# Running the maximum scores three units ahead, with the maxima sent as two transfers of one row

## The chip, the core and the metric

The kernel runs on one core of a Trainium2 chip: TensorE (PE) for matrix products, VectorE (DVE), ScalarE (ACT) and GpSimd (POOL) for elementwise work, and SyncE (SP) and ACT's queue to issue transfers. The metric is device time in microseconds for one execution, median of several runs.

## What is computed

32 sequences of 128 tokens with 128 features go through a self attention, a cross attention to a second sequence, a gate and a gated MLP, with a padding mask on the keys of both attentions. There are 16 heads of 8 features.

```python
def masked_attn(q, k, v, valid_keys):
    scores = jnp.einsum('bhqd,bhkd->bhqk', q, k) / math.sqrt(HD)
    scores = jnp.where(valid_keys[:, None, None, :], scores, jnp.finfo(scores.dtype).min)
    return jnp.einsum('bhqk,bhkd->bhqd', jax.nn.softmax(scores, axis=-1), v)
# tokens: rmsnorm, film, q/k/v, rope on q and k
tokens = tokens + merge_heads(masked_attn(q, k, v, valid)) @ out_w.T + out_b
# cross: query = rmsnorm(tokens), keys and values from rmsnorm(seq_tokens)
attended = merge_heads(masked_attn(cq, ck, cv, svalid)) @ mha_out_w.T + mha_out_b
update = attended * valid_rows
gate = jax.nn.sigmoid(jnp.concatenate([tokens, update], axis=-1) @ gate_w.T + gate_b)
tokens = tokens + gate * update
g, val = jnp.split(rmsnorm(tokens, ffn_norm_w) @ gu_w.T + gu_b, 2, axis=-1)
out = tokens + jax.nn.silu(g) * val @ down_w.T + down_b
```

## The kernel before

**Tiling.** The 32 sequences form 8 groups of 4. Each group passes one self phase and one cross phase, so there are 16 phases, in the order of the table `ORDER` (L35: SELF 0 to 3, CROSS 0, SELF 4, CROSS 1 and so on, the last three being CROSS 5, 6 and 7). A phase has four *units* (one sequence each, 64 in all), a unit has four *quarters* of four heads (256 in all), and two units make a *pair* (32 in all).

**Order.** Every engine runs its own program, and all of them walk through the same loop over quarters, `for t in range(FIRST, LAST)`, with `n, q = divmod(t, 4)`. What an engine does in a quarter is written out by hand through due times: `s_prep(g)` and `c_prep(g)` start the preparation of a group's self and cross phase, `top_time(m)` is the quarter in which the maxima of pair m are turned, `post(g, step)` and `mlp(g)` place what follows the attention. An engine takes its work strictly in this order; semaphores hold it until its inputs are there.

**Attention.** q and k are cut into three bfloat16 parts each, and the nine products of parts are stacked along the partitions: `q_st` and `k_st` (`st`, three sets, one per phase in turn) have 72 rows of parts, a row for the mask, and in `q_st` two rows for the maxima. The stacks are filled by transfers from SP (`stack`, L658; three for each part, 18 in a phase). The parts themselves (`part_q`, `part_k`) are written by ACT (`keep_hi`, L872, and `keep_mid`, L876) and POOL. `keep_hi` waits (`parts_free`) until the transfers of an earlier phase have landed, since it overwrites what they read.

Scores are made twice. `max_scores(n, q)` (L356, matmuls L366) makes scores with queries on the partitions in `ps_a`; DVE reduces them to a maximum for each query and head (`maxima`, L1087) in `top`. This runs `LEAD` units ahead, 4 before the change: in quarter t PE makes the maximum scores of quarter t + 16. `prob_scores(n, q)` (L378, L386) makes them again with keys on the partitions in `ps_b`, the two rows of the maxima being part of the contraction, so that the maximum is already taken off; ACT's exponential (`exps`, L902) writes `probs`, and `weigh` (L390, L403) multiplies them with the values one unit later.

**The maxima of a pair** go this way: DVE splits them, negated, into two bfloat16 parts (`split_tops`, L1096 and L1098, `top_part`); PE turns them (`turn_tops`, L374) into a PSUM bank; ACT copies them (`keep_top`, L888) to `top_t`, 32 partitions (2 parts by 16 heads) of 256 queries; ACT's queue issues the transfer (`top_rows`, L895) that lays them as two rows of `q_st`. `prob_scores` waits for it at the first quarter of every second unit, that is at quarter 8m for pair m. In the kernel before, the split of pair m is at quarter 8m-8, the turn at 8m-5 (8m-7 for pair 0), copy and transfer at 8m-4, the copy ahead of that quarter's exponential and the transfer behind it.

**DVE beside this.** At the last quarter of every second unit `take_pair` (L1105, L1107) takes a pair's output; `divide_pair`, `keep_v`, `rope` and the norms have their own quarters. **ACT beside this:** in each quarter, after its exponential, copies and squares (L828), L863, L922 and L924. **PE:** within a quarter it does `weigh` (third quarter of a unit), `turn_tops`, `max_scores`, `prob_scores`, then the quarter's products.

Of the kernel before, what the change touches and what calls it, by code (L numbers as in the profile page):

```python
# [14 lines left out]
H = 16  # L15
# [14 lines left out]
TOPS = 2  # L30
# [9 lines left out]
POS = {one: p for p, one in enumerate(ORDER)}  # L40
LEAD = 4
SETS = 3
# [5 lines left out]
def s_prep(g):  # L48
    return 16 * (POS[SELF, g] - 2) - 8 - 6 * (g == 1)

# [23 lines left out]
def top_time(m):  # L74
    return 8 * m - (7 if m == 0 else 5)

# [33 lines left out]
def build(nc, x, side, cond, mask, anw, qkv_w, qkv_b, out_w, out_b, film_w, film_b, sqw, snw, in_w, in_b,  # L110
          mo_w, mo_b, gate_w, gate_b, fnw, gu_w, gu_b, down_w, down_b, cos_t, sin_t, ident_t, out):
    with ExitStack() as ctx:
# [189 lines left out]
        def _(pe):  # L302
# [75 lines left out]
            def prob_scores(n, q):  # L378
                p, b = divmod(n, NG)
                i = p % SETS  # L380
                if q == 0:
                    pe.wait_ge(top_in[n // 2 % 2], 16 * (n // 4 + 1))
                wait(pe, exp_done, NQ * n + q - 1)
                for j in range(QH):
                    h = QH * q + j
                    mm = pe.matmul(ps_b[q % 2][:, j * S:(j + 1) * S], st[1][i][0:R_END, h, b * S:(b + 1) * S],  # L386
                                   st[0][i][0:R_END, h, b * S:(b + 1) * S], start=True, stop=True)
                mm.then_inc(b_done, 1)
# [419 lines left out]
        def _(act):  # L808
# [76 lines left out]
            def keep_top(m):  # L885
                src = full_in(act, ("top", m))
                wait(act, top_in[m % 2], 16 * (m // 2))
                act.activation(top_t[:, m % 2, :], src[:, :].bitcast(BF16)[0:TOPS * H, 0:2 * S], ACT.Copy  # L888
                               ).then_inc(taken_sem(("top", m)), 1)

            def top_rows(m):

                p, pair = divmod(m, 2)
                taken(act, ("top", m))
                act.dma_start(st[0][p % SETS][R_MAX:R_END, :, pair * 2 * S:(pair + 1) * 2 * S], top_t[:, m % 2, :]  # L895
                              ).then_inc(top_in[m % 2], 16)

# [64 lines left out]
            for t in range(FIRST, LAST):  # L962
                n, q = divmod(t, 4)
                for m in range(PAIRS):
                    if t == top_time(m) + 1:
                        keep_top(m)
                if 0 <= n < UNITS:
                    exps(n, q)
                for m in range(PAIRS):
                    if t == top_time(m) + 1:  # L970
                        top_rows(m)
                for g in range(G):
# [64 lines left out]
        def _(dve):  # L1037
# [198 lines left out]
            for t in range(FIRST, LAST):  # L1236
                n, q = divmod(t, 4)
                if n % 2 == 0 and q == 0 and 0 <= (n + 2) // 2 < PAIRS:
                    split_tops((n + 2) // 2)
                if 0 <= n + LEAD < UNITS:  # L1240
# [90 lines left out]
```

## Time and profile before

| | |
|---|---|
| median of 3 runs | 515.77 us (515.37 to 520.08) |
| the profiled execution | 517.94 us, span 516.1 us |
| PE busy | 442.1 us, 86% of the span |
| DVE busy | 350.1 us, 68% |
| ACT busy | 290.4 us, 56% |
| POOL busy | 190.8 us, 37% |
| mean granted TensorE clock | 0.937 |

The profile shows one execution. "Busy" is the time in which an engine executes; the wait of an engine is told by the instruction that ends it and by what released it. PE's granted clock is a share of 2.4 GHz: 1.0 is that level, 0.5 is the lower level of 1.2 GHz, and a value between them is a mean over a stretch that had both. The first 41 us of the span are preparation; from there to 61 us PE makes the maximum scores of the first four units and prepares other groups; the last phase's scores end at 479 us, and the rest is the MLP of the last group.

### The profile page before, as it was taken

To read this page: it belongs to the slowest core of one execution; us is meant where nothing else is said; L and a number is where in the kernel's file an instruction comes from. 1 tells how busy PE (TensorE), PEld (TensorE's weight loads), DVE (VectorE), ACT (ScalarE), POOL (GpSimd) and SP (SyncE) were. 2 spreads that over 40 slices of the span, in tenths; PEclk is the share of its full clock that TensorE was granted. 3 is DMA by queue.
4 is the path that set the end of the run, shared out by engine and by line. 5 is a ranking of instruction groups with operands and counts; after the bars stand their busy time and mean duration, and the time that the engine had idled before them with its cause. 6 is when DMAs were issued, how large, how long until landed. Compare 5 with 4: busy or idle time off the path is not lost.

```text
span 516.1 us, 13226 instructions
## 1 busy us (share of the span) xinstructions
PE 442.1 (86%) x5219; PEld 308.3 (60%) x5219; DVE 350.1 (68%) x655; ACT 290.4 (56%) x644; POOL 190.8 (37%) x184
## 2 busy tenths in 40 slices
PE   3546889878897986999989988999999969999897
PEld 2115375756675664666577655866586748565664
DVE  2326655878885896698677866767748856856565
ACT  4321364577566664777576648486636744556243
POOL 4451140614433163528381828254542542000010
PEclk9975778899997999799999999999989999999999
DMA  3355442354353445344443443425140320000001
GB/s 77 87 174 174 131 122 88 100 162 151 100 162 107 140 121 153 103 128 121 131 137 108 117 140 97 153 67 163 43 149 25 98 92 3 23 3 22 22 1 42
DMA packets 62942, 52.04 MB, mean 101 GB/s; under 512 B 3803, under 2 KB 61728, under 8 KB 62880
## 3 DMA queue, kind: packets, MB, share of 16 engines
q1 hardware_dynamic: 60050, 49.07, 32.2%
q10 hardware_dynamic: 2830, 2.12, 1.4%
q8 instruction: 42, 0.69, 0.6%
q14 instruction: 20, 0.16, 0.1%
HBM read 8.55 MB, written 2.11 MB: 21 GB/s over the span
## 4 chain that ended last, share of the span: by engine, by line
PE 52%; DVE 11%; DMA 10%; ACT 8%; issue 8%; SPq 5%; POOL 4%; ACTq 1%; DVEq 0%; POOLq 0%
PE ps_o L403 8%; PE ps_a L366 7%; PE ps_g L320 7%; PE ps_b L386 6%; PE ps_g L461 5%; SPq L658 4%; DMA k_st<-part_k 4%; DVE top L1087 4%; PE ps_g L444 4%; PE ps_g L353 3%; DMA q_st<-top_t 3%; ACT probs L902 2%; DMA s_in<-in_fside_BxSxS 1%; ACT turned_in L838 1%; PE ps_g L418 1%
## 5 line engine op out<-in xcount | busy, mean ns | idle before, releaser
L1087 DVE TENSOR_REDUCE top<-ps_a 128x4 f32<-128x512 f32 x256 | 169.6, 680 | 106.1 <-PE ps_a L366 104.8
L902 ACT ACTIVATE probs<-ps_b 128x512 f32<-128x512 f32 x256 | 151.3, 595 | 143.6 <-PE ps_b L386 139.5
L366 PE MATMUL ps_a<-k_st,q_st 73*128 73x128 bf16 x1024 | 105.0, 228 | 27.8 <-DMA k_st<-part_k 15.0
L366 PEld LDWEIGHTS ps_a<-k_st,q_st 73*128 73x128 bf16 x1024 | 69.8, 101 | 79.5 <-issue 59.9
L386 PE MATMUL ps_b<-q_st,k_st 75*128 75x128 bf16 x1024 | 102.0, 223 | 9.4 <-ACT probs L902 7.5
L386 PEld LDWEIGHTS ps_b<-q_st,k_st 75*128 75x128 bf16 x1024 | 69.6, 99 | 18.5 <-issue 9.2
L403 PE MATMUL ps_o<-probs,v_pad 128*32 128x128 f32 x2048 | 73.3, 287 | 0.0
L403 PEld LDWEIGHTS ps_o<-probs,v_pad 128*32 128x32 f32 x2048 | 55.3, 115 | 24.1 <-issue 14.7
L728 POOL TENSOR_TENSOR f<-f 128x4 f32<-128x4 f32 x16 | 16.6, 1038 | 98.8 <-DVE f L1136 98.8
L320 PE MATMUL ps_g<-norm,w_t 128*128 128x512 f32 x66 | 37.1, 647 | 1.2 <-DVE hid L1178 1.2
L320 PE MATMUL ps_g<-turned_in,w_t 128*128 128x512 f32 x48 | 30.3, 717 | 5.0 <-ACT turned_in L838 4.8
L444 PE MATMUL ps_g<-norm,w_t 128*128 128x512 f32 x56 | 30.1, 620 | 3.3 <-DVE quotient L1132 2.6
L461 PE MATMUL ps_g<-w_t,hid 128*128 128x128 f32 x224 | 27.4, 276 | 0.0
L765 POOL TENSOR_SCALAR unit_th<-unit_th 128x512 f32<-128x512 f32 x16 | 9.9, 620 | 45.0 <-ACT unit_th L922 45.0
L461 PEld LDWEIGHTS ps_g<-w_t,hid 128*128 128x128 f32 x224 | 26.0, 192 | 0.0
L922 ACT ACTIVATE unit_th<-ps_g,half_g_b 128x512 f32<-128x512 f32 x22 | 15.1, 686 | 14.3 <-PE ps_g L444 14.3
L1105 DVE STREAM_TRANSPOSE turned<-ps_o 128x512 f32<-128x512 f32 x32 | 22.6, 706 | 0.3 <-PE ps_o L403 0.3
L749 POOL TENSOR_TENSOR part_k<-full_k,part_k 128x512 bf16<-128x512 f32 x14 | 16.2, 1158 | 17.8 <-ACT part_k L876 17.7
L353 PE MATMUL ps_g<-w_t,turned_in 128*128 128x128 f32 x128 | 21.9, 325 | 0.2 <-ACT top_t L888 0.2
L718 POOL TENSOR_TENSOR f<-f 128x4 f32<-128x4 f32 x16 | 16.4, 1024 | 14.5 <-DVE f L1043 13.9
L744 POOL TENSOR_TENSOR full_k<-full_k,part_k 128x512 f32<-128x512 f32 x14 | 16.4, 1168 | 13.3 <-ACT part_k L872 13.3
L768 POOL TENSOR_TENSOR hid<-hid,unit_th 128x512 f32<-128x512 f32 x16 | 20.3, 1268 | 1.3
(197 smaller groups left out, 677.6 us busy)
## 6 DMA issues: line engine op xcount, KB each, us to landing
q_st<-part_q SPq DMA_DIRECT2D x126, 128.0 KB
k_st<-part_k SPq DMA_DIRECT2D x120, 128.0 KB
x_in<-in_x SPq DMA_DIRECT2D x16, 256.0 KB, 4.5
q_st<-hid SPq DMA_DIRECT2D x18, 128.0 KB
s_in<-in_fside_BxSxS SPq DMA_DIRECT2D x8, 256.0 KB, 5.7
out<-t SPq DMA_DIRECT2D x8, 256.0 KB, 2.3
k_st<-hid SPq DMA_DIRECT2D x12, 128.0 KB
swap_q<-part_q SPq DMA_DIRECT2D x8, 128.0 KB, 2.3
```

Of the source, the lines that this page charges most:

```text
L320: pe.matmul(to[:, :], w, rhs, start=True, stop=True).then_inc(done, 1)
L353: mm = pe.matmul(to[:, b * D:(b + 1) * D], src[:, b * S:(b + 1) * S], w, start=True, stop=True)
L366: mm = pe.matmul(ps_a[q % 2][:, j * S:(j + 1) * S], st[0][i][0:R_MAX, h, b * S:(b + 1) * S], st[1][i][0:R_MAX, h, b * S:(b + 1) * S], star ...
L386: mm = pe.matmul(ps_b[q % 2][:, j * S:(j + 1) * S], st[1][i][0:R_END, h, b * S:(b + 1) * S], st[0][i][0:R_END, h, b * S:(b + 1) * S], star ...
L403: mm = pe.matmul(ps_o[32 * c:32 * c + 32, u * 256:(u + 1) * 256].rearrange("p (b r q) -> p r b q", r=2, q=32)[:, r], v_pad[p % 2][:, b, at ...
L444: pe.matmul(to[:, :], w_t[:, W_GU + j, :], norm3[:, :], start=True, stop=True).then_inc(done, 1)
L461: mm = pe.matmul(to[:, b * D:(b + 1) * D], hid[:, j, b * S:(b + 1) * S], w_t[:, W_DOWN + j, :], start=False, stop=j == 3 and b == NG - 1)
L658: sp.dma_start(st[r][p % SETS][product:R_MASK:PRODUCTS, :, :], parts(r, p)[:, o, :]).then_inc(stacked[r][p % 2], 16)
L768: pool.tensor_tensor(hid[:, j, :], hid[:, j, :], unit_th[:, :], ALU.mult).then_inc(g_mul, 1)
L902: act.activation(probs[:, n % 2, q * T:(q + 1) * T], ps_b[q % 2][:, :], ACT.Exp, scale=SCALE).then_inc(exp_done, 1)
L1087: dve.tensor_reduce(top[:, n // 2 % 2, n % 2, QH * q:QH * (q + 1)], ps_a[q % 2][:, :].rearrange("p (h k) -> p h k", h=QH), AX.X, ALU.max). ...
L1105: dve.transpose(turned[:, :], ps_o[:, :]).then_inc(o_taken, 1)
```

## The change

The maximum scores run three units ahead (`LEAD = 3`). The preparation of SELF 2 is moved by four quarters to keep its place to the maximum scores that read it. The split of pair m goes from quarter 8m-8 to 8m-4, ahead of that quarter's maxima, the turn to 8m-3 for every pair, copy and transfer to 8m-2. The transfer is cut into two of one row each, 16 partitions of `top_t` for each, and both are issued ahead of the quarter's exponential. The waits count two transfers for each pair.

```diff
-LEAD = 4
+LEAD = 3
 def s_prep(g):
-    return 16 * (POS[SELF, g] - 2) - 8 - 6 * (g == 1)
+    return 16 * (POS[SELF, g] - 2) - 8 - 6 * (g == 1) + 4 * (g == 2)
 def top_time(m):
-    return 8 * m - (7 if m == 0 else 5)
+    return 8 * m - 3
...
                 if q == 0:
-                    pe.wait_ge(top_in[n // 2 % 2], 16 * (n // 4 + 1))
+                    pe.wait_ge(top_in[n // 2 % 2], 16 * TOPS * (n // 4 + 1))
...
                 src = full_in(act, ("top", m))
-                wait(act, top_in[m % 2], 16 * (m // 2))
+                wait(act, top_in[m % 2], 16 * TOPS * (m // 2))
...
                 taken(act, ("top", m))
-                act.dma_start(st[0][p % SETS][R_MAX:R_END, :, pair * 2 * S:(pair + 1) * 2 * S], top_t[:, m % 2, :]
-                              ).then_inc(top_in[m % 2], 16)
+                for part in range(TOPS):
+                    act.dma_start(st[0][p % SETS][R_MAX + part:R_MAX + part + 1, :, pair * 2 * S:(pair + 1) * 2 * S],
+                                  top_t[H * part:H * part + H, m % 2, :]).then_inc(top_in[m % 2], 16)
...
                 for m in range(PAIRS):
                     if t == top_time(m) + 1:
                         keep_top(m)
+                        top_rows(m)
                 if 0 <= n < UNITS:
                     exps(n, q)
-                for m in range(PAIRS):
-                    if t == top_time(m) + 1:
-                        top_rows(m)
...
-                if n % 2 == 0 and q == 0 and 0 <= (n + 2) // 2 < PAIRS:
-                    split_tops((n + 2) // 2)
+                if n % 2 == 1 and q == 0 and 0 <= (n + 1) // 2 < PAIRS:
+                    split_tops((n + 1) // 2)
```

## Rows read from the trace of the kernel before

**Rows 1.** Waits of PE from 61 us on: us, times, longest
```profile
PE ps_b L386 <- ACT probs L902: 7.5, 16, 0.9
PE ps_a L366 <- DMA k_st<-part_k: 7.1, 2, 4.4
PE ps_a L366 <- DVE top L1087: 6.5, 11, 1.6
PE ps_a L366 <- issue: 3.9, 1, 3.9
PE ps_g L425 <- ACT norm L931: 3.5, 5, 0.8
...
PE ps_b L386 <- DMA q_st<-top_t: 1.9, 3, 1.1
```

**Rows 2.** The chain that ended last, one piece: start us, us, what
```profile
119.79 3.46 DMA q_st<-top_t
```

**Rows 3.** Timeline behind two stack waits: start us, us, instruction [idle before]
```profile
157.72 0.63 ACT L872 ACTIVATE part_k<-full_k 128x512 bf16<-128x512 f32 x1 [2.35 <-DMA k_st<-part_k]
...
160.93 0.63 PE L386 MATMUL ps_b<-q_st,k_st 75*128 75x128 bf16 x4
...
206.67 0.63 ACT L872 ACTIVATE part_k<-full_k 128x512 bf16<-128x512 f32 x1 [3.47 <-DMA k_st<-part_k]
...
209.88 0.63 PE L386 MATMUL ps_b<-q_st,k_st 75*128 75x128 bf16 x4
```

**Rows 4.** Stretch behind the third wait: length, busy time by engine, PE's clock, DMA
```profile
424.00:427.00 3.00, 3.00 (x46) 2.38 (x45) 1.21 (x2) 2.24 (x4) 1.41 (x2) 0.55 0.02 5
```

**Rows 5.** Instructions on `top` (ns min/median/max), and the page's group of maximum scores
```profile
L1087 DVE TENSOR_REDUCE top<-ps_a x256: 627/683/693, 41.4 to 450.1; 128x4 f32<-128x512 f32 x128
L1096 DVE TENSOR_SCALAR top_part<-top x32: 171/182/933, 49.0 to 450.9; 128x32 bf16<-128x32 f32 x32
L1098 DVE SCALAR_TENSOR_TENSOR top_part<-top,top_part x32: 191/193/1075, 49.2 to 451.1; 128x32 bf16<-128x32 f32 x32
...
L366 PE MATMUL ps_a<-k_st,q_st 73*128 73x128 bf16 x1024 | 105.0, 228 | 27.8 <-DMA k_st<-part_k 15.0
```

**Rows 6.** Timeline around pair 5, by ACT, DVE and PE
```profile
119.41 0.36 ACT L888 ACTIVATE top_t<-ps_g 32x256 bf16<-32x256 bf16 x1
119.67 0.57 ACT L902 ACTIVATE probs<-ps_b 128x512 f32<-128x512 f32 x1
...
120.49 0.60 ACT L902 ACTIVATE probs<-ps_b 128x512 f32<-128x512 f32 x1 [0.25 <-issue]
...
119.04 0.11 DVE L1043 TENSOR_SCALAR f<-f 128x4 f32<-128x4 f32 x1
...
118.17 0.40 PE L366 MATMUL ps_a<-k_st,q_st 73*128 73x128 bf16 x4
```

**Rows 7.** Timeline at pair 1 (ACT, PE) and pair 30 (DVE, PE), first and last late
```profile
71.37 0.19 ACT L828 ACTIVATION_READ_ACCUMULATOR junk<-x_in 128x1 f32 x1
...
73.48 0.39 PE L386 MATMUL ps_b<-q_st,k_st 75*128 75x128 bf16 x4
...
444.83 0.63 DVE L1087 TENSOR_REDUCE top<-ps_a 128x4 f32<-128x512 f32 x1
...
444.60 0.39 PE L366 MATMUL ps_a<-k_st,q_st 73*128 73x128 bf16 x4
```

**Rows 8.** Issue of the maxima (ns min/median/max), and a mask row at 255 us (us to landing)
```profile
L895 ACTq DMA_DIRECT2D q_st<-top_t x32: 621/621/697, 50.3 to 459.7; - x32
...
k_st<-mask_rows SPq DMA_DIRECT2D x1, 16.0 KB, 2.2
```

**Rows 9.** Timeline around pair 22, by ACT and PE
```profile
338.55 0.22 ACT L828 ACTIVATION_READ_ACCUMULATOR junk<-s_in 128x1 f32 x1
...
339.40 0.38 PE L386 MATMUL ps_b<-q_st,k_st 75*128 75x128 bf16 x4 [0.69 <-ACT probs L902]
```

## The prediction

> **What bounds the kernel now.** I read the page's busy times first (PE is the busiest engine, by the table above), then PE's waits from 61 us on, where the first probability scores are made. The reader is to see in them that little is left idle, and where [rows 1]. Three long waits stand out, all at the first maximum scores of a phase (`max_scores` with b == 0, q == 0, which waits for the stacked operands): two of 7.1 us together, the longer 4.4 us, and one of 3.9 us named "issue". The third has the same place (first quarter of the last phase) and nothing else to wait for, so I take it to be the same wait. The row of the maxima itself costs little: 1.9 us in three waits, and when PE waits for it, it lands 3.46 us after its issue [rows 1, 2]. The rest is short and spread: 7.5 us on ACT's exponentials, 6.5 us on DVE's maxima, 3.5 us on a square.
>
> A quarter t below is one turn of the loops; pair m needs its maxima at quarter 8m.
>
> **What the change gives.** Maximum scores run 12 quarters ahead of the probability scores and no longer 16, while the stacking of a phase stays where it was (but for SELF 2, moved by 4). So each phase's stacks get four quarters, some 6 us, more before the first reader. All three waits are shorter than that.
> - The 3.9 us wait: nothing else waits for those stacks, all of it goes. 3.9.
> - The wait of 4.4 us: ACT's L872 (the next phase's copy) waits for the same landing until 206.67 and ends at 207.30; the exponential behind it then ends at 207.9, and the probability scores two quarters later need it. They began at 209.88 and can't begin before 207.8 [rows 3]. 2.1.
> - Its sister of 2.7 us (7.1 less 4.4): the same, L872 at 157.72, its exponential done at 158.9, the scores it holds at 160.93 [rows 3]. 2.0.
> - A small one at the fourth phase turns into a wait for the maxima; 0.2.
> That is 8.2 us. After such a wait PE runs at the lower level for a while: granted clock 0.55 in the 3 us after the last, so 1.35 us lost [rows 4]. I give all of that back once and half of it, 0.9 in all, for the two waits that only shrink: 2.3.
> - Start: four quarters of maximum scores, paced by DVE at 0.68 us each while nothing else runs, no longer stand ahead of the first probability scores: 2.7. They come at the end instead, where PE is full, at 105.0/256 = 0.41 us a quarter [rows 5]: minus 1.6. Net 1.1. The preparation of SELF 2, moved by four quarters, leaves the start and comes back just behind it; nothing.
> Gain in all: 8.2 + 2.3 + 1.1 = 11.6 us.
>
> **What it costs.** The time from the last maximum to the first reader of the row shrinks from 8 quarters to 4.
> 1. *The split.* `split_tops(m)` now runs at quarter 8m-4, right behind the quarter whose maxima it needs; in that same quarter DVE also has `take_pair` (L1105, L1107). `turn_tops` on PE comes one quarter later, at 8m-3, where it had three. Behind it in PE's order wait that quarter's maximum and probability scores. The split itself takes 0.18 + 0.19 us, 0.42 with the handover [rows 5]. Pair 5: DVE is free at 119.1, the split would be there at 119.5, PE reached that quarter at 118.17: 1.3 us late [rows 6]. The last such is pair 30: DVE takes the next maximum at 444.83, the split would be there at 445.25, PE is there at 444.60: 0.65 [rows 7].
> 2. *The landing.* The copy `keep_top` goes to quarter 8m-2, behind everything ACT has in 8m-3, and the transfers are issued at once, ahead of the exponential. From the end of ACT's work of 8m-3 it takes 0.39 (copy, to the issue) + 0.55 (first issue) + the landing of the second. The before kernel's issue takes 0.62 [rows 8]; for a one-row one I estimate 0.55. The landing lies between 2.2 us, which a one-row transfer on a quiet queue takes (the mask row) and 3.46 (the maxima beside stacks) [rows 2, 8]. I take 2.3, near the lower end: the transfer has ACT's queue to itself. So 3.24 us after ACT is free. Pair 22: ACT ends with 8m-3 at 338.77, so 342.0; the scores began at 339.40: 2.6 late [rows 9]. Pair 1, the first late one: ACT is through at 71.56; but copy and issue no longer stand ahead of the exponentials before it, which held them up by 0.26 us (copy at 119.41, exponential at 119.67) and by some 0.3 (idle 0.25 for the issue) [rows 6], so 70.96; landing 74.2 against 73.48: 0.7 late [rows 7].
>
> The Trainium skill (DMA: Bandwidth & Descriptors, "Why a DMA increments its semaphore by 16 and not by 1") says that a transfer is spread over the largest number of engines up to 16 that divides both outermost sizes: two for the old one (32 rows to 2), sixteen for each of the new ones; it speaks for a landing near the lower bound, as I take it by the rows.
>
> Done for all 31 pairs in this way (later of the two paths, less what the exponentials gain), 22 are late, pair 1 the first and pair 30 the last, by 30.0 us in sum: 12.7 from the split, 17.3 more from the landing. The two issues hold the exponential of 8m-2 by about 1.5 us, but its result, copy + issues + 0.6 = 2.1 us after ACT is free, is there before the landing; while that cover stands it costs nothing more. A late pair isn't lost whole: PE has 17.5 us of short waits [rows 1] which the others can fall into while PE stands. I let a third be swallowed: 20.0 us remain.
>
> **The sum.** 516.1 - 11.6 + 20.0 = 524.5 for the profiled span. The profiled execution itself took 517.94, the median of the runs is 515.77; I put the difference on the median: 515.77 + 8.4 = 524.2 us.
>
> **Rivals.**
> - *Stalls mostly swallowed, same.* If half of the 30.0 goes, 15 - 11.6 = +3.4, 519.2. For it: the late pairs cluster in the first half, where PE's short waits are; against: after 250 us PE is full and pairs 20, 22 and 26 are late by 2.3 to 2.6 each. 0.25.
> - *Faster.* DVE, freed from lagging by PE's pauses, has the split ready when PE comes, and the row lands in 2 us. It decides from 0.53 us for each of 22 late pairs downward (11.6/22), and is faster by over 1% below 0.3. At 0.2 each: 4.4 - 11.6 = -7.2, 508.6. For it: the waits for the stacks are certain and the lateness is an inference; against: ACT's work ahead of the copy is real, and 2.3 is already the low end. 0.20.
> - *The rows land no sooner than now.* With 3.3 us, just under the 3.46 of the row [rows 2], the same list sums to 50.4: 33.6 - 11.6 = +22, 537.8. For it: the stacks load the DMA engines in most of the span. 0.07. The Trainium skill says so for halves (DMA: Bandwidth & Descriptors, "Rules for kernel authors"): don't cut a transfer into two over disjoint partitions, they serialize on the same engines. No run yet shows it for these shapes.
> - *The stack waits stay*, because L872 keeps ACT waiting for them and all else behind it [rows 3]: the gain falls to the last wait, its clock and the start, 3.9 + 1.4 + 1.1 = 6.4: +13.6, 529.4. 0.08.
> My forecast: 0.40.
>
> **How the numbers follow.** Faster 0.20; within 1% (about what a measurement of this kernel can tell from no change) 0.25; slower 0.40 + 0.07 + 0.08 = 0.55. The forecast alone, with landings of 2.3 to 2.8 us (sum 38.8, so up to 530) and a swallowed share of a third to 45%, spans 520 to 530. The range goes down to half of the faster case and up past the case of the stacks: 509 to 533; below it I leave some 0.1, above it 0.1.
>
> **What would show it.** Right: PE's waits for `k_st` after 61 us fall under 4 us in sum and the 3.9 us one is gone; `turn_tops` (L374) appears as a waiter on DVE's `top_part` with some 8 to 13 us; PE's L386 waits on the transfer of `top_t` for 8 to 20 us; first probability scores near 54 us and not 61. Wrong: L374 and L386 wait under 7 us together, then it is faster; or `k_st` waits as long as before; or PE's clock falls after the new stalls, which I count at nothing.

## The result and the profile after

| | before | changed |
|---|---|---|
| median | 515.57 us (4 runs) | 601.83 us (4 runs) |
| ratio, 95% interval | | 1.164 [1.157, 1.170] |
| profiled execution | 517.94 us, span 516.1 | 600.95 us, span 599.2 |
| PE busy in the span | 442.1 us | 475.4 us |
| PE idle from 61 us on, pauses over 50 ns | 44.7 us | 90.1 us |
| mean granted TensorE clock | 0.937 | 0.880 |

The direction was forecast, the size was not: 86 us lost where 8.4 were predicted, far above the range. The table says where they are. PE ran the same 5219 instructions and was busy 33.3 us longer; its pauses grew by 45.4 us. Together that is 78.7 of the 83.1 us of span. Ratios, here and below, leave out executions that took over 1.5% longer than the fastest of their kernel.

The first lines of the page of the changed kernel, its row of the granted clock and its queues (q10 is ACT's, with the rows of the maxima; before it had 2830 packets):

```profile
span 599.2 us, 13258 instructions
PE 475.4 (79%) x5219; PEld 329.2 (55%) x5219; DVE 357.0 (60%) x655; ACT 290.0 (48%) x644; POOL 190.1 (32%) x184
...
PEclk9775788869996889897889889888879989979999
...
q10 hardware_dynamic: 3790, 2.13, 1.4%
```

PE's waits in the changed kernel from 61 us on (line, what ended the wait, us in total, times, longest), to be read against [rows 1]:

```profile
PE ps_g L374 <- DVE top_part L1097: 18.4, 17, 2.1
PE ps_b L386 <- DMA q_st<-top_t: 18.1, 13, 2.9
PE ps_g L353 <- DVE hid L1177: 10.3, 6, 3.0
PE ps_g L374 <- DVE norm L1141: 5.5, 4, 1.6
PE ps_g L444 <- DVE hid L1177: 4.2, 2, 2.2
PE ps_b L386 <- ACT probs L903: 4.1, 4, 2.0
PE ps_g L439 <- ACT full_k L863: 4.1, 3, 1.4
PE ps_a L366 <- DVE top L1086: 3.7, 9, 0.8
```

Three things are to be seen. The three waits for the stacks of [rows 1] are gone. The first two rows are the two new waits that I predicted: the turn on the split, the scores on the landing of the rows. And the third, fourth, fifth and seventh rows stand in no line of the prediction. They end when DVE or ACT has read out an earlier result in `ps_g`, the PSUM banks that all small products share: `hid` is DVE's read of an MLP product, `norm` DVE's second half of a normalisation, `full_k` ACT's read of a key product. PE waits there for a bank and not for data. Before, L353, the values' product, waited 0.6 us in the whole kernel.

A stretch of the changed kernel, PE alone (start, duration, instruction, in brackets the idle time before it and its releaser):

```profile
352.90 0.27 PE L374 MATMUL ps_g<-ident_b,top_part 128*128 128x128 bf16 x2 [1.55 <-DVE norm L1141]
...
354.98 2.05 PE L439 MATMUL ps_g<-t,w_t 128*128 128x512 f32 x2 [1.36 <-ACT full_k L863]
356.82 1.91 PE L440 MATMUL ps_g<-upd,w_t 128*128 128x512 f32 x2
358.66 1.94 PE L403 MATMUL ps_o<-probs,v_pad 128*32 128x128 f32 x32
```

The granted clock over it (stretch; its length; busy time and count of PE, PEld, DVE, ACT, POOL; PE's clock; DMA share; GB/s):

```profile
351.00:355.00 4.00, 1.09 (x12) 0.63 (x11) 3.29 (x7) 1.41 (x5) 0.45 (x1) 0.83 0.19 54
355.00:360.00 5.00, 5.00 (x32) 2.37 (x36) 0.57 (x1) 0.37 (x3) 0.00 (x0) 0.50 0.03 7
360.00:363.00 3.00, 3.00 (x39) 2.05 (x32) 1.50 (x3) 1.81 (x5) 0.55 (x1) 0.92 0.00 1
```

Two pauses for banks, 1.55 and 1.36 us, in a stretch in which PE was busy 1.09 of 4 us, and behind them 5.9 us of matmuls (2.05, 1.91, 1.94) at a granted clock of 0.50, the lower level of 1.2 GHz; the same three groups took 1.10, 1.02 and 1.08 us in the kernel before. So the two pauses of 2.9 us were followed by 2.7 us more of PE's time for the same work. This is how 33 us of busy time come from the same instructions.

### The profile page after: what moved, and what is told of

The parts are those of the page before. It is cut to its first block, busy times and chain, and to the rows that moved or that the text cites. A ratio compares the mean times of both kernels' runs of the same rounds, so it can differ in the third digit from the quotient of the medians.

```text
span 599.2 us, 13258 instructions
## 1 busy us (share of the span) xinstructions
PE 475.4 (79%) x5219; PEld 329.2 (55%) x5219; DVE 357.0 (60%) x655; ACT 290.0 (48%) x644; POOL 190.1 (32%) x184
## 4 chain that ended last, share of the span: by engine, by line
PE 50%; DVE 17%; issue 8%; DMA 8%; ACT 7%; POOL 4%; ACTq 3%; SPq 2%; DVEq 0%; POOLq 0%
PE ps_o L403 9%; DMA q_st<-top_t 7%; PE ps_g L320 6%; PE ps_a L366 6%; DVE top L1086 6%; PE ps_b L386 6%; PE ps_g L461 4%; PE ps_g L444 4%; PE ps_g L353 3%; DVE turned L1104 2%; SPq L658 2%; PE ps_g L338 1%; DMA t<-in_L_cond_down_w 1%; DVE top_part L1097 1%; PE ps_g L439 1%
## 5 line engine op out<-in xcount | busy, mean ns | idle before, releaser
L386 PE MATMUL ps_b<-q_st,k_st 75*128 75x128 bf16 x1024 | 106.3, 229 | 26.3 <-DMA q_st<-top_t 21.8
L366 PE MATMUL ps_a<-k_st,q_st 73*128 73x128 bf16 x1024 | 108.8, 234 | 14.8 <-DMA k_st<-part_k 8.6
L366 PEld LDWEIGHTS ps_a<-k_st,q_st 73*128 73x128 bf16 x1024 | 73.2, 104 | 60.3 <-issue 47.2
L386 PEld LDWEIGHTS ps_b<-q_st,k_st 75*128 75x128 bf16 x1024 | 73.0, 103 | 35.1 <-DMA q_st<-top_t 24.5
L403 PE MATMUL ps_o<-probs,v_pad 128*32 128x128 f32 x2048 | 83.3, 313 | 0.0
L403 PEld LDWEIGHTS ps_o<-probs,v_pad 128*32 128x32 f32 x2048 | 62.1, 125 | 29.3 <-issue 17.9
L320 PE MATMUL ps_g<-norm,w_t 128*128 128x512 f32 x68 | 39.1, 661 | 0.7 <-ACT probs L903 0.7
L353 PE MATMUL ps_g<-w_t,turned_in 128*128 128x128 f32 x128 | 26.5, 373 | 14.5 <-DVE hid L1177 10.3
L444 PE MATMUL ps_g<-norm,w_t 128*128 128x512 f32 x56 | 32.2, 658 | 4.8 <-DVE hid L1177 4.2
L353 PEld LDWEIGHTS ps_g<-w_t,turned_in 128*128 128x128 f32 x128 | 23.0, 269 | 15.8 <-DVE hid L1177 9.0
L374 PE MATMUL ps_g<-ident_b,top_part 128*128 128x128 bf16 x64 | 9.4, 232 | 27.3 <-DVE top_part L1097 19.0
L374 PEld LDWEIGHTS ps_g<-ident_b,top_part 128*128 128x128 bf16 x64 | 4.1, 99 | 39.7 <-DVE top_part L1097 27.5
L749 POOL TENSOR_TENSOR part_k<-full_k,part_k 128x512 bf16<-128x512 f32 x14 | 16.2, 1156 | 29.9 <-ACT part_k L876 29.8
L718 POOL TENSOR_TENSOR f<-f 128x4 f32<-128x4 f32 x16 | 16.4, 1024 | 17.8 <-DVE f L1042 17.3
```

The costliest lines, as they stand in the source:

```text
L320: pe.matmul(to[:, :], w, rhs, start=True, stop=True).then_inc(done, 1)
L353: mm = pe.matmul(to[:, b * D:(b + 1) * D], src[:, b * S:(b + 1) * S], w, start=True, stop=True)
L366: mm = pe.matmul(ps_a[q % 2][:, j * S:(j + 1) * S], st[0][i][0:R_MAX, h, b * S:(b + 1) * S], st[1][i][0:R_MAX, h, b * S:(b + 1) * S], star ...
L403: mm = pe.matmul(ps_o[32 * c:32 * c + 32, u * 256:(u + 1) * 256].rearrange("p (b r q) -> p r b q", r=2, q=32)[:, r], v_pad[p % 2][:, b, at ...
L444: pe.matmul(to[:, :], w_t[:, W_GU + j, :], norm3[:, :], start=True, stop=True).then_inc(done, 1)
L718: pool.tensor_tensor(r[:, :], ms[:, :], minus_half[:, :], ALU.pow).then_inc(root_set, 1)
```

## The experiments

"Lead 4" below means `LEAD = 4` and the old due time of SELF 2. Each diff is against the kernel it is named for; a ratio is to the kernel before on the same chip. The kernel before had medians of 512.3, 518.1, 514.9 and 513.8 us beside the four groups of runs, which ran on three chips; where kernels of two groups are compared, or a single execution is given, some 5 us are not certain. Kernels without the landing's wait or without the turn leave out a part of the computation; they serve for timing alone.

### One part alone: the cut

Kernel before, only the transfer cut in two, both still at quarter 8m-4 behind the exponential.

```diff
-                act.dma_start(st[0][p % SETS][R_MAX:R_END, ...], top_t[:, m % 2, :]).then_inc(top_in[m % 2], 16)
+                for part in range(TOPS):
+                    act.dma_start(st[0][p % SETS][R_MAX + part:R_MAX + part + 1, ...],
+                                  top_t[H * part:H * part + H, m % 2, :]).then_inc(top_in[m % 2], 16)
```

> The kernel before with only the transfer cut into two of one row each, still at quarter 8m-4 and behind the exponential; lead 4. Theory A (lateness in the chain of the maxima makes the loss, the transfers themselves are cheap): within 1% of before, perhaps 1 to 2 us faster since PE's three waits for the maxima shrink. Theory B (thirty-two more issues on ACT and 16 instead of 2 engines for each disturb the stacks): slower by 2% or more.

Measured: 515.16 against 512.29 us, ratio 1.003 [0.997, 1.008]. Where nobody waits for the rows, the cut costs nothing that can be measured.

### Turn and landing late, lead 4

Changed kernel with lead 4; the turn at 8m-3 and copy and transfers at 8m-2 ahead of the exponential, as changed, but the split at its old quarter 8m-8.

```diff
-LEAD = 3
+LEAD = 4
...
-                if n % 2 == 1 and q == 0 and 0 <= (n + 1) // 2 < PAIRS:
-                    split_tops((n + 1) // 2)
+                if n % 2 == 0 and q == 0 and 0 <= (n + 2) // 2 < PAIRS:
+                    split_tops((n + 2) // 2)
```

> Lead 4, split at quarter 8m-8 as before, but turn at 8m-3 and copy and two transfers at 8m-2 ahead of the exponential, as in the changed kernel. Theory A1 (the late landing is the main part): 550 us or more, PE waits over 15 us for the transfer of top_t. Theory A2 (the split right behind its maxima is the main part): under 535 us. Theory C (the later turn changes which PSUM bank each product gets, and the bank waits are the loss): L353 and L439 wait on DVE and ACT as in the changed kernel, some 20 us.

Measured: 576.98 us (one execution; the kernel before 512.29 on that chip), granted clock 0.884. More than 60 us of the loss are there without the shorter lead and without the late split. PE waits 20.6 us for the rows and 12.4 us at L353 for DVE's `hid`, much as in the changed kernel: the waits for banks come with the moved turn and not with the shorter lead.

### All of it late, lead 4

As the last one, but with the split at 8m-4 as in the changed kernel; only the lead and SELF 2 are undone.

```diff
-LEAD = 3
+LEAD = 4
-    return 16 * (POS[SELF, g] - 2) - 8 - 6 * (g == 1) + 4 * (g == 2)
+    return 16 * (POS[SELF, g] - 2) - 8 - 6 * (g == 1)
```

> The changed kernel with lead 4 and the old due time of SELF 2: only the chain of the maxima is late (split 8m-4, turn 8m-3, copy and transfers 8m-2). Theory A (all of the loss lies in that chain): 600 us or a little more, since the stack waits of 11 us come back. Theory D (the shorter lead itself costs, by the order of products on PE): clearly under 590 us.

Measured: 593.42 us (one execution), clock 0.870, 16 us above the last one: the late split, with 16.8 us of waits of L374 for `top_part`. The maximum scores here run four units ahead, as before, and still no wait for `k_st` over 0.2 us is left. So these waits don't need a shorter lead to go: once PE walks slower, the stacks are there in time. The gain I credited to lead 3 was a gain against a pace that the kernel no longer had.

### The landing's wait taken away

Changed kernel, but the probability scores contract over the 73 rows without the maxima and so wait for no landing. The transfers are still issued; SP waits for them at the end.

```diff
-                    pe.wait_ge(top_in[n // 2 % 2], 16 * TOPS * (n // 4 + 1))
...
-                    ... st[1][i][0:R_END, ...], st[0][i][0:R_END, ...]
+                    ... st[1][i][0:R_MAX, ...], st[0][i][0:R_MAX, ...]
...
-                ... ACT.Exp, scale=SCALE
+                ... ACT.Exp, scale=SCALE / 256
```

> The changed kernel with probability scores that do not read the two rows of the maxima and do not wait for their transfer (the maxima are not taken off; the exponential's scale is 1/256 of its value so that nothing overflows); SP waits for the transfers at the end. All else is kept. Theory A1: the 21.8 us of PE's waits for the transfer go, and with them part of the low clock: 565 to 575 us. Theory A2 or C: 585 us or more, because PE then waits as long for the split or a bank.

Measured: 581.22 us (one execution), clock 0.900, between the two expectations. The landing is worth some 20 us (14 if each kernel is taken as a ratio to the kernel before on its own chip); three quarters of the loss are elsewhere. L374 waits 19.5 us for the split, L353 10.9 us for a bank.

### Only the transfers late

Kernel before with everything in its place (lead, split, turn and its bank, copy), only the transfer cut in two, as in the first experiment, and moved to 8m-2, ahead of the exponential.

```diff
+                    if t == 8 * m - 2:
+                        top_rows(m)
...
-                for m in range(PAIRS):
-                    if t == top_time(m) + 1:
-                        top_rows(m)
```

> The kernel before (lead 4, split 8m-8, turn 8m-5, copy 8m-4, so the PSUM banks go as before) with the two one-row transfers alone moved to quarter 8m-2, ahead of its exponential: only the landing is late. Theory A1 (the landing's lateness, about 20 us of PE waits and the low clock behind them, is the main part of the loss): 545 us or more. Theory C (the banks, not the landing, carry most): under 530 us.

Measured: 528.8 against 518.05 us, ratio 1.020 [0.999, 1.040]; the interval just touches no change. L386 waits 13.4 us for the rows in 12 waits (from 61 us on; before 1.9 in 3) and PE is busy 451.9 us instead of 442.1. This is the loss that my prediction describes, a landing that comes too late: some 11 us by the medians (the interval goes from 0 to 21), where the prediction has 17.3 us of lateness, two thirds of it left. With PE's bank of the turn left where it was, there is no wait at L353.

### The bank's part, lead 4

The lead 4 kernel with the late turn and the early split, without the landing's wait (the diffs of the second and the fourth experiment together).

> The kernel of e2 (lead 4, split early, turn 8m-3, copy and transfers 8m-2) whose probability scores leave out the two rows of the maxima and do not wait for them (exponential's scale 1/256): what is left of the change is the place of turn and copy, and with it the banks. e2 took 577 us. Theory A1: 535 us or less. Theory C: 555 us or more, with L353 still waiting over 10 us for DVE.

Measured: 547.59 against 518.05 us, ratio 1.056 [1.032, 1.080], between the two expectations. Neither the split nor the landing can be late here, and PE's longest waits (from 57 us on) are these:

```profile
PE ps_b L386 <- ACT probs L904: 12.4, 19, 2.2
PE ps_g L353 <- DVE hid L1178: 11.6, 6, 3.0
PE ps_a L366 <- DVE top L1087: 9.4, 12, 1.6
PE ps_g L439 <- ACT full_k L864: 4.1, 3, 1.4
```

The stretches say where. The first seven phases of probability scores take 167.7 us here and 168.4 us in the kernel before; the next eight take 249.6 and 222.3. The whole loss lies from the eighth phase on, where the MLP's products are, and where L353 and an MLP product meet.

### Neither the landing's nor the split's wait

Changed kernel, lead 3, the landing's wait left out as above; PE turns a constant instead of `top_part` and so doesn't wait for the split. The turn still takes its bank at 8m-3, and ACT still reads it.

```diff
-                pe.wait_ge(top_split, m + 1)
...
-                    mm = pe.transpose(to[:, :].bitcast(BF16)[:, u * S:(u + 1) * S], top_part[:, m % 2, u, :],
+                    mm = pe.transpose(to[:, :].bitcast(BF16)[:, u * S:(u + 1) * S], ident_b[:, :],
```

> The changed kernel without both waits of the maxima's chain: the scores do not read the rows nor wait for them, and PE turns the identity in place of the split maxima and does not wait for the split (scale 1/256). Left: lead 3, places, banks, DVE's and ACT's work. e4, with the split's wait, took 581 us. Theory A: near 530 us. Theory C (banks): 560 us or more.

Measured: 562.39 us, ratio 1.084 [1.066, 1.103]. With both predicted costs gone, 44 us remain. L353 waits 14.5 us for DVE's `hid`, the turn itself 5.1 us for DVE's `norm`.

### The values' product three quarters earlier

`v_time(p)` is 16(p-1)+5, which is 8m-3 for every second pair: the very quarter to which the turn was moved. Here it goes three quarters earlier.

```diff
-    return 16 * (p - 1) + 5
+    return 16 * (p - 1) + 2
```

> The changed kernel with v_time three quarters earlier (16(p-1)+2), so that the values' product no longer asks for a PSUM bank in the very quarter of a turn; by the order in which the banks are given out, the takes of a bank that is not yet due free fall from 19 to 14 and the four of the values behind a value unit of the MLP go. Theory C: L353's waits for DVE's hid (14.5 us with all) vanish and the time falls by 20 us or more, to 580 us or less. Theory A: within 8 us of 601.

Measured: 597.26 us (a second execution, left out as said above, 610.21), inside the changed kernel's own 596.5 to 605.0. PE's waits (from 57 us on):

```profile
PE ps_b L386 <- DMA q_st<-top_t: 29.1, 20, 3.0
PE ps_g L374 <- DVE top_part L1097: 25.7, 20, 3.2
PE ps_g L425 <- ACT norm L932: 11.1, 8, 2.6
```

The waits of L353 are gone, as was expected, and the time is not: the pauses turn up at the split (25.7 us against 18.4), at the landing (29.1 against 18.1) and at L425 (11.1 against 3.5). The delays hide parts of one another, and taking away this one alone gave nothing back; taking away the landing alone did (20 us, above).

### PE kept busy in its new pauses

Changed kernel with 16 extra score matmuls ahead of every wait for the split and every wait for the landing, 992 in all. They overwrite nothing that is still read. The wait for the exponentials goes ahead of them.

```diff
+                wait(pe, exp_done, NQ * n + q - 1)
                 if q == 0:
+                    if n % 2 == 0:
+                        for j in range(16):
+                            pe.matmul(ps_b[0][:, j % 4 * S:(j % 4 + 1) * S], st[1][i][0:R_MAX, j, ...],
+                                      st[0][i][0:R_MAX, j, ...], start=True, stop=True)
                     pe.wait_ge(top_in[n // 2 % 2], 16 * TOPS * (n // 4 + 1))
-                wait(pe, exp_done, NQ * n + q - 1)
...
                     if t == top_time(m):
+                        if 0 < n < UNITS - LEAD:
+                            ...
+                            for j in range(16):
+                                pe.matmul(ps_a[q % 2][:, j % 4 * S:(j % 4 + 1) * S], ...)
                         turn_tops(m, t)
```

> The changed kernel with 16 extra score matmuls (0.9 us at the full clock, results overwritten) put on PE ahead of each wait for the split and ahead of each wait for the maxima's transfer. Theory F (PE's idle time lowers its granted clock, and this low clock is a third or more of the loss): mean clock rises from 0.88 to 0.93 or more and the time falls below 590 us although PE does 56 us more work. Theory G (the clock falls for another reason, or its loss only fills slack): 610 us or more.

Measured: 599.18 us, ratio 1.163 [1.155, 1.172], the same as the changed kernel, and between the two expectations. PE is busy 509.0 us, 33.6 more, and its pauses shrink by as much, from 90.1 to 55.7 us; the granted clock rises from 0.880 to 0.922. The filler alone takes 68.6 us of PE, while the kernel's own 5219 matmuls need 455.2 us instead of 475.4. So the filler is paid for twice, out of the pauses (34 us) and out of what the higher clock gives back (20 us; the rest overlaps other matmuls), and the time stays. The run shows that the pauses lower the clock. It can't show how much of the clock's 33 us of busy time is lost time: at many pairs PE had no wait there, or a shorter one than the filler's 1.1 us, and the filler costs time, and where the chain from split to landing bounds a pair, a faster PE would only wait longer.

### One transfer instead of two

Changed kernel, one transfer of both rows, still ahead of the exponential.

```diff
-                for part in range(TOPS):
-                    act.dma_start(st[0][p % SETS][R_MAX + part:R_MAX + part + 1, ...],
-                                  top_t[H * part:H * part + H, m % 2, :]).then_inc(top_in[m % 2], 16)
+                act.dma_start(st[0][p % SETS][R_MAX:R_END, ...], top_t[:, m % 2, :]).then_inc(top_in[m % 2], 16)
```

> The changed kernel with the old single transfer of two rows, issued at the same place (8m-2, ahead of the exponential). If a one-row transfer lands 1 us or more earlier than the two-row one under load, every late pair pays: 615 us or more. If the cut brings nothing (e1, where the transfer is not waited for, showed no difference): within 5 us of the changed kernel's 602.

Measured: 587.93 us, ratio 1.141 [1.134, 1.149]: 14 us faster than the changed kernel (12 by the ratios), which neither expectation had. The two issues, in the changed kernel:

```profile
L896 ACTq DMA_DIRECT2D q_st<-top_t x64: 510/606/1086, 50.2 to 542.8; - x64
```

and the one of this kernel (count; shortest, median, longest ns; first and last start):

```profile
L895 ACTq DMA_DIRECT2D q_st<-top_t x32: 620/621/696, 48.5 to 529.4; - x32
```

A half costs nearly as much to issue as the whole. With idle DMA engines (pairs 14, 18, 22 and 26, PE waiting in both kernels) the scores begin 2.47 to 2.48 us after the first issue with two transfers and 2.32 to 2.41 us after the only one: nearly even. Beside the stacks' transfers the cut is late: 6.23 against 5.08 us for pair 9, 3.33 against 2.30 for pair 8, 4.48 against 3.91 for pair 7 (and 3.20 against 3.19 for pair 4). By pair 14 the kernel with one transfer is 12.8 us ahead (244.81 against 257.65 us), which is the whole difference of the two spans (586.3 and 599.2). The stacks load the DMA engines behind it too, and landings of 3.9 to 4.5 us come there as well (pairs 15, 17, 19, 21, 23 and 25), but at those pairs PE isn't waiting. From pair 14 on it waits at 14, 18, 22 and 26, on nearly idle engines, and at pair 28 for 0.78 us.

### SELF 2 left where it was

```diff
-    return 16 * (POS[SELF, g] - 2) - 8 - 6 * (g == 1) + 4 * (g == 2)
+    return 16 * (POS[SELF, g] - 2) - 8 - 6 * (g == 1)
```

> The changed kernel with SELF 2's preparation at its old due time. The first phase lasts 36.7 us in the changed kernel and 28.7 before. If the moved preparation makes this (its q and k products and rope beside the late weights): 5 to 8 us less, near 595 us. If it is the late maxima: no change, 600 to 606 us.

Measured: 597.96 us, ratio 1.161 [1.154, 1.168]. The first phase takes 26.6 us instead of 36.7, but starts 2.5 us later, and the later phases give back over half of the 7.6 us that are left: 4 us in all (1 to 2 by the ratios).

### The clock after the stack waits of the kernel before

Kernel before with 48 extra matmuls ahead of each of the three long waits for stacks.

```diff
+                    if p in (5, 7, 15):
+                        wait(pe, max_done, NQ * n + q - 1)
+                        for j in range(48):
+                            pe.matmul(ps_a[0][:, j % 4 * S:(j % 4 + 1) * S], st[0][(p - 1) % SETS][0:R_MAX, j % H, 0:S],
+                                      st[1][(p - 1) % SETS][0:R_MAX, j % H, 0:S], start=True, stop=True)
```

> The kernel before with 48 extra matmuls (2.7 us at the full clock) on PE ahead of its waits for the stacks of phases 5, 7 and 15, which last 2.7 to 4.4 us. Theory F: the clock no longer falls behind these waits (0.50 to 0.55 in the 3 us after them), 3 to 6 us faster than before. Theory G: no change or slightly slower.

Measured: 514.62 against 514.91 us, ratio 0.999 [0.995, 1.004]. The stretch of [rows 4] in this kernel:

```profile
424.00:427.00 3.00, 3.00 (x36) 2.13 (x34) 2.96 (x6) 2.53 (x6) 0.72 (x1) 1.00 0.01 2
```

The clock is 1.00 instead of 0.55 (the work in this stretch lies some 4 us further on, but in the 3 us right behind the wait it is 1.00 too, against 0.51), and the median is the same. But the interval goes from 2.7 us faster to 1.8 slower, so it neither shows nor excludes the 2.3 us that my prediction gave back for the clock. The traces say more. From the first scores behind the wait to the maximum scores 12 quarters on, PE takes 14.42 us with the filler and 16.38 without it in phase 7, and 18.58 against 20.01 in phase 15 (numbered as in the diff); the 2.0 and 1.4 us are made in the first two quarters. In phase 5 a pause of 2.07 us was left in spite of the filler, the clock in the 3 us behind it was 0.50 in both, and both take 16.2 us. So the price of the clock behind such a wait is there, 1.4 us at the last one, where I had read 1.35.

### Without the turn and its bank

Changed kernel without the landing's wait and without `turn_tops`: PE makes no turn and takes no bank for it, ACT's copy reads a constant, after the split, and DVE's split no longer waits for a turn two pairs back.

```diff
-                        turn_tops(m, t)
...
-                src = full_in(act, ("top", m))
+                act.wait_ge(top_split, m + 1)
...
-                act.activation(top_t[:, m % 2, :], src[:, :].bitcast(BF16)[0:TOPS * H, 0:2 * S], ACT.Copy
-                               ).then_inc(taken_sem(("top", m)), 1)
+                act.activation(top_t[:, m % 2, :], ident[0:TOPS * H, :].bitcast(BF16), ACT.Copy).then_inc(top_kept, 1)
```

> The changed kernel in which the chain of the maxima takes no PSUM bank: PE does not turn (0.3 us of PE for each pair left out), ACT copies a piece of the identity into top_t at the same place once the split is done, both transfers go as changed, the scores neither read the rows nor wait for them (scale 1/256). e7, the same with a turn and its bank, took 562 us. By the order in which banks are given out, all takes of the values, gate and MLP that came too early go (19 to 9). Theory C (banks): 525 us or less. Theory P (ACT's and DVE's work of the chain at its new place): 550 us or more.

Measured: 527.33 us, ratio 1.026 [1.018, 1.034], close to theory C. That is 35 us below the kernel that has the turn and its bank (562.39), or 30 us by the ratios, as the two ran on different chips. PE's 64 turning matmuls themselves account for little of it: 32 groups of 0.27 us, 8.6 us if all of them were on the path. Nor does ACT's wait for the turn: in the kernel that has it, ACT waited for it once, 1.1 us. The rest, 21 to 26 us (each of the two ratios is certain to 1 or 2%, 5 to 10 us), is the bank. The values' product (L354 here) waits 0.2 us for `hid` in all, and the gate (L440 here) no longer waits for `full_k`; the longest waits from 57 us on are of other kinds:

```profile
PE ps_b L387 <- ACT probs L904: 15.2, 24, 2.2
PE ps_g L426 <- ACT norm L933: 11.9, 8, 3.4
PE ps_a L367 <- DVE top L1087: 7.6, 16, 0.8
PE ps_g L440 <- DVE norm L1140: 3.3, 3, 1.1
```

### The same with lead 4

The last kernel with lead 4, SELF 2 at its old due time and the split at 8m-8.

> The same with lead 4 and the early split: e6 (548 us) without turn and bank. Theory C: 512 us or less, about 35 us off. Theory P: 540 us or more. Beside e13 it gives the price of lead 3 alone: with theory L (the shorter lead gains what the stack waits cost) e13 is 5 us or more faster than this one.

Measured: 522.13 us, ratio 1.016 [1.009, 1.024], 10 us above what theory C expected. Lead 3 with its later split and SELF 2's move does not gain here: together they cost 5 us, although on PE nothing waits for split, turn or landing in either kernel. Against the kernel before, 8 us are left, and PE waits longer for the exponentials (14.7 us against 7.5) and, at the means (L426 here, L425 before), for `norm` (11.9 against 3.5). What makes them longer was not taken apart.

### One transfer, behind the exponential

Changed kernel with the single transfer put back behind the quarter's exponential (the diff is against the kernel with one transfer).

```diff
                         keep_top(m)
-                        top_rows(m)
                 if 0 <= n < UNITS:
                     exps(n, q)
+                for m in range(PAIRS):
+                    if t == top_time(m) + 1:
+                        top_rows(m)
```

> The changed kernel with the single two-row transfer, behind the exponential of 8m-2 as the kernel before has it. e10, with it ahead, took 588 us. If the order matters: 5 us or more above e10, since the issue waits for that quarter's scores. If not: within 4 us.

Measured: 613.06 us, ratio 1.193 [1.181, 1.205], 25 us above the single transfer ahead of it. L386 waits 33.3 us for the rows in 25 waits, against 10.3 us in 9.

### What the runs add up to

Each step below the second row changes one thing, or two that go together, against the one above it:

| kernel | us | ratio | step |
|---|---|---|---|
| before | 512 to 518 | 1 | |
| copy and transfers late, no turn, no bank, no landing's wait, lead 4 | 522 | 1.016 | +8 |
| with the turn and its bank at 8m-3 | 548 | 1.056 | +20 to 25 |
| with the landing's wait | 577 | 1.128 (one execution) | +29 to 37 |
| with the split at 8m-4 | 593 | 1.160 (one execution) | +16 |
| lead 3 and SELF 2: the changed kernel | 602 | 1.164 | +2 to 8 |

The kernels ran in different groups; of each two bounds one comes from the times as they are and one from the ratios. The order matters too, since the delays hide one another: the bank was worth 20 to 25 us in this ladder and 30 to 35 us measured from the other end, the landing 29 to 37 us here and 14 to 21 us when it was taken out of the changed kernel, the split 16 us here and 19 to 27 us taken out behind it. The turn's own matmuls, up to 8.6 us, are in the bank's step and missing in the one above it.

**How the bank comes to matter.** The small products take their `ps_g` bank from three in turn. The kernel plans this ahead: each product states until which quarter it holds its bank, and the next in the order takes the one that is due to be released first. With the turn at 8m-3 a product is added in the quarter of the values' product. Counted in that plan, products that get a bank ahead of the quarter planned for its release are about as many as before (19 against 18), but of another kind: four times a values' product gets the bank of an MLP product that DVE (L1177) still reads, three times the gate (L439) gets one that ACT (L863) reads. In the trace these are among L353's six waits for `hid`, of up to 3.0 us, and L439's three, of up to 1.4 us. What was not tried is another fix than an earlier values' product, such as a bank that belongs to the turn alone; that such a kernel would be quick is argued, not shown. None of the kernels tried beats the kernel before beyond its interval.

## Why the prediction was right and wrong

**Right: the two late steps.** The split was predicted to be late by 12.7 us in sum; L374 waits 18.4 us for `top_part`. Pair by pair the working held where nothing else intervened: pair 5 waits 1.31 us at the turn where 1.3 was worked out, pair 30 0.47 where 0.65. The landing was predicted with 17.3 us more; L386 waits 18.1 us. That these two agree is luck in part: 6.1 of the 18.1 us are waits of four pairs that landed in 1.9 us, and the other 12 come at nine pairs whose second transfer landed after 2.6 to 6.7 us, where 2.3 was assumed. Pair 22 was worked out as 2.6 us late [rows 9], and this is what it looks like after, first ACT, then PE's first score:

```profile
394.22 0.36 ACT L888 ACTIVATE top_t<-ps_g 32x256 bf16<-32x256 bf16 x1
394.61 1.16 ACTq L896 DMA_DIRECT2D q_st<-top_t  x2
395.81 0.60 ACT L903 ACTIVATE probs<-ps_b 128x512 f32<-128x512 f32 x1 [1.24 <-issue]
```

```profile
397.07 0.40 PE L386 MATMUL ps_b<-q_st,k_st 75*128 75x128 bf16 x4 [2.86 <-DMA q_st<-top_t]
```

Copy, two issues of 0.52 and 0.61 us, a landing 1.87 us after the start of the second; the scores wait 2.86 us. Of the marks under "What would show it", the stack waits (under 4 us) and L386 (8 to 20 us) came out, L374 with 18.4 us was above its 8 to 13, and the first scores came at 57.2 us and not near 54, because they waited 3.7 us for the rows of pair 0; without that wait it would have been 53.5. The mechanism was there, and most of the time was lost elsewhere.

**Wrong, first: the moved turn's bank.** The step "`turn_tops` on PE comes one quarter later" was costed only by when its input is there. That the turn also takes one of three PSUM banks, and so changes which product waits for which reader, stood nowhere in the sum. It was worth about as much as the whole landing: 20 to 25 us with lead 4, where it lies in the phases with the MLP (the first seven phases of scores take 165.7 us without it and 167.7 with it, the next eight 225.5 and 249.6), and 30 to 35 us with lead 3; up to 8.6 us of each are the turn's own matmuls, which the changed kernel did not add.

**Wrong: the clock, which the prediction names and counts at nothing.** It took the fallen clock behind the old waits from [rows 4] and gave it back as a gain, and put no such charge on the new ones. The new pauses are many, and behind the two shown above PE runs at 0.50: 5.9 us of work that took 3.2 before. Over the kernel PE is busy 33.3 us longer for the same instructions. The filler in the changed kernel raised the clock but used up what that gave back, so I can't say how many of the 33 us the clock alone costs.

**Wrong: "a third be swallowed".** The 30.0 us of lateness were to shrink to 20.0, as PE's other waits fall into the new ones. The three rows of short waits did shrink, but by 6.2 us and not by 10, from 17.5 to 11.3 (4.1 for the exponentials, 3.7 for the maxima, 3.5 for `norm`). Against that stands the slower PE: measured, the split's step cost 16 to 27 us and the landing's 14 to 37, by the place at which it is taken away, against 12.7 and 17.3 of lateness. With banks as before and the transfers alone late, the waits for the rows grew by 11.5 us, PE was busy 9.8 us longer, and the span of the profiled execution grew by 13.5.

**Wrong: the gain of 11.6 us.** The 8.2 us of stack waits were real [rows 3] and are gone, but they also go with lead 4 once PE is slower, so they can't be counted against the stalls. The 2.3 us for the clock are too small for the medians (the filler in the kernel before: ratio 0.999 [0.995, 1.004]); its trace shows 2.0 and 1.4 us behind two of the three waits. So this term stands, and what failed was to leave the same price out of the costs. Of the start, the first probability scores came at 57.20 us instead of 61.01, where about 54 was forecast; and "the preparation of SELF 2 comes back just behind it; nothing" failed: the first phase of scores took 36.7 us instead of 28.7. In the end lead 3 and SELF 2's move together cost 2 to 8 us, of which SELF 2's old place gives back up to 4; that the shorter lead by itself costs anything is not shown.

**Wrong in part: the cut.** "I take 2.3, near the lower end: the transfer has ACT's queue to itself." A quiet landing was 1.9 us, better than that, but over all it was 2.6 us in the median and up to 6.7:

```profile
DMA to landing us min/median/max: 1.8/2.6/6.7
```

The chain that ended last has twelve of these landings in the changed kernel; three of them (start, us), two loaded and one quiet:

```profile
102.72 4.58 DMA q_st<-top_t
...
183.57 5.63 DMA q_st<-top_t
...
255.73 1.87 DMA q_st<-top_t
```

The kernel before has such landings too. Its chain holds three, and [rows 2] show only the shortest; the other two are

```profile
107.70 5.95 DMA q_st<-top_t
...
166.41 4.03 DMA q_st<-top_t
```

So "it lands 3.46 us after its issue" and the upper bound of 3.46 misread the trace that was at hand: the transfer has its queue to itself but not the DMA engines, which the stacks use at the same time. The rival "the rows land no sooner than now", given 0.07, was nearer with its 537.8 us and right in its mechanism for the loaded pairs, though it too explains only a part. The Trainium skill (DMA: Bandwidth & Descriptors, "Rules for kernel authors") advises against two transfers to disjoint halves; the runs agree where someone waits (12 to 14 us) and show no cost where nobody does (ratio 1.003). Its rule on the spread (same page, "Why a DMA increments its semaphore by 16 and not by 1") is in line with the 30 more packets for each pair, 960 in all in q10; that a wider spread lands no sooner when each of the engines has stacks in its line is my reading of the loaded pairs and was not isolated, since spread and number of transfers changed together.

## What to carry to other kernels

When a piece of work is moved to another quarter, list what it takes out of a shared pool there (here one of three PSUM banks) and who reads the bank that it or its neighbour gets next; the arrival of its own input is only a part of its cost. Stalls in front of a dense engine are not to be discounted for overlap alone: here the short waits took in 6 us, and the lower clock that came with the stalls added 33 us of busy time. When a cost is read from one row, look at every row of its kind: the landing read as 3.46 us was 5.95 and 4.03 us in the same chain. And a wait that a change removes counts as a gain only if it would still be there at the pace that the change leaves.

## What was not expected of the hardware

- Two pauses of 1.55 and 1.36 us close together (PE busy 1.09 of 4 us) were followed by 5 us at a granted clock of 0.50; a sequence of 5.9 us took 3.2 us in the other kernel.
- Work that keeps PE busy ahead of a wait holds the clock (0.55 to 1.00 in one stretch of the kernel before, 0.880 to 0.922 in the mean of the changed one) and the median of neither moved beyond its interval; in the first one's trace PE was 2.0 and 1.4 us quicker behind two waits.
- A one-row transfer of 16 partitions takes 0.51 to 1.09 us to issue from ACT, a two-row one of 32 partitions 0.62 to 0.70 us: cutting a small transfer nearly doubles the issue time (1.16 us for the two of pair 22).
- The same small transfer lands after 1.8 us on quiet DMA engines and after up to 6.7 us beside the stacks.
